# Spreading the reciprocal denominators by DMA in the linear-attention stage of a decoder layer

## The chip, the core and the metric

The kernel runs on one core of a Trainium2 chip. The metric is the device time of one launch in microseconds (us). Its engines are PE (matmuls, with the weight loads as PEld), DVE (vector), ACT (scalar), POOL (GpSimd) and SP, which here only issues DMAs. Each engine runs its own instructions in program order and waits on semaphores.

## The reference, cut to what matters

One decoder layer in fp32 on x of shape (2, 2048, 512): linear attention, cross attention over 154 context tokens, and a mixture of experts, each behind a layer norm and with a residual. The change touches the linear attention alone:

```python
qkv = x @ w_qkv                                   # 16 heads of 32
q_proj = _elu1(einsum('bhnd,hdf->bhnf', q, proj_matrix))     # 128 features
k_proj = _elu1(einsum('bhnd,hdf->bhnf', k, proj_matrix))
kv = einsum('bhnf,bhnd->bhfd', k_proj, v)
attn = einsum('bhnf,bhfd->bhnd', q_proj, kv)
z = 1.0 / (einsum('bhnf,bhf->bhn', q_proj, k_proj.sum(axis=2)) + 1e-08)
out = (attn * z[..., None]) @ w_out + b_out
x = x + out
```

The next stage's queries, `layernorm(x) @ Wq.T + bq`, are made in the same loop.

## The kernel before

Four stages follow each other: `project` (the projections and the sums over keys, up to about 424 us), `attend_linear` (424 to 742 us), `attend_cross` and `experts`. The tokens are cut into 8 blocks of 512 (`TB`); a block has 4 groups of 4 heads (`G`, `HG`). An fp32 product is made of three matmuls with parts called HI and LO (`PASSES`), so a tile of 128x512 over 512 inputs takes 12 matmuls.

`attend_linear` is a software pipeline written out by hand. `turns(slot)` calls every engine's `slot(i, s, ahead, now, behind)` for bodies i = -1 to 8 and slots s = 0 to 7. In body i three blocks are worked on: the features of block i+1 ("ahead"), the normalisation, output projection and layer norm of block i ("now"), and the cross-attention queries of block i-1 ("behind"). Each slot begins with two heads: PE makes a head's product in one of three banks (L1166), ACT makes relu and exp (L1003, L1006), DVE joins them (L1086). After its two heads PE runs the jobs that `PLAN[s]` lists:

- ND g (L1176, L1182): the denominators (`p_den`) and numerators (`p_num`) of a group of four heads. ND 3 of block i stands in slot 0 of body i; then all denominators of the block are there.
- R g (L1191, `spread_out`): the reciprocals, which lie in 16 of the 128 partitions, are spread over the 32 partitions of each head by a matmul with a matrix of ones and zeros, HI and LO.
- O t (L1204, `out_proj`): the output projection of 128 tokens, 12 matmuls; group g of its input needs `norm_lo` of that group.
- T t (L1213): four transposes of the layer-normed tokens.
- XQ g (L1226, `queries`): a 128-row part of the queries of block i-1, 12 matmuls.

R, O, T and XQ share three banks in the order in which they come; a job waits until the one three places before has been read. The denominators go: ACT copies them with 1e-8 added (`take_den`, L960), DVE takes the reciprocal in two halves (L1049), ACT and POOL split it into HI and LO (L965, L924), PE spreads it (R), DVE multiplies the numerators by it (`normalise`, L1054), ACT makes HI of the product (`normalised`, L971), POOL makes LO (L936, `norm_lo`), and O may begin.

A finished XQ g is read by ACT (`query`, L989) and DVE (L1091) into one of two buffers, `xq[:, g % 2]`, which SP writes to DRAM (`query_out`, L874). ACT's `query(m, g)` for g = 2 and 3 waits until the write of g - 2 of the same block has landed (`xq_out[g % 2]`). SP issues all DMAs of the loop, in its own program order: `query_out`, `load_q` (L186, the queries of the linear attention two blocks ahead), the store and the load of x.

## Time and profile before

| | us |
|---|---|
| median of 3 runs | 2382.08 |
| lowest, highest | 2378.66, 2383.08 |
| profiled execution | 2380.94 |
| its span | 2379.2 |
| PE busy in the span | 2278.0 |
| attend_linear in the span | about 424 to 742 |

The page gives each engine's busy time over the whole span; the views by stretch and the timeline give it for one body of the loop. A granted clock of 1.00 is TensorE's higher level (2.4 GHz), 0.50 its lower one (1.2 GHz). Times in a timeline are from the start of the span. A wait is put down to the event that came last.

### The profile page before, as it was taken

Reading aid. Unit: us, or ns where it says so; the run is one execution under the profiler, and the core shown is the slowest. Engines: PE = TensorE matmul, PEld = TensorE weight load, DVE = VectorE, ACT = ScalarE, POOL = GpSimd, SP = SyncE. Lnnn points to the kernel's source line nnn. Section 1 sums busy time; section 2 is a strip of 40 time slices with the busy share of each in tenths; the row PEclk is TensorE's granted clock in tenths of the full one; section 3 lists DMA queues with packets and bytes.
Section 4 is the critical chain, followed back from the end, with each engine's and each line's share of the span. In section 5 each row is a group of like instructions: output and inputs, shape, how many; then the busy total and the mean of one; then the engine's idle time right before and its main releaser. Section 6 shows DMA issues by size and latency. Waiting matters only on the chain.

```text
span 2379.2 us, 34267 instructions
## 1 busy us (share of the span) xinstructions
PE 2278.0 (96%) x12200; PEld 1775.7 (75%) x12200; DVE 1390.5 (58%) x2258; ACT 1158.5 (49%) x2745; POOL 838.9 (35%) x820
## 2 busy tenths in 40 slices
PE   7999999899998899998799999999999999999998
PEld 6888886566666566665588878888788887888887
DVE  5555456777774668777644466444664445644444
ACT  3555566767663767774544444333343333433332
POOL 1444345333341245545677762111111111111111
PEclk9999999999999899999899999999999999999999
DMA  7655546666646457784656546454345543464442
GB/s 209 161 146 128 134 107 157 210 187 195 177 142 181 102 145 188 185 225 138 217 174 212 177 141 214 171 177 142 129 153 201 177 142 125 136 215 139 140 139 77
DMA packets 140218, 387.46 MB, mean 163 GB/s; under 512 B 15920, under 2 KB 38064, under 8 KB 123440
## 3 DMA queue, kind: packets, MB, share of 16 engines
q1 hardware_dynamic: 139760, 384.77, 53.9%
q8 instruction: 98, 1.61, 0.3%
q10 hardware_dynamic: 288, 0.49, 0.1%
q14 instruction: 72, 0.59, 0.1%
HBM read 254.00 MB, written 104.07 MB: 151 GB/s over the span
## 4 chain that ended last, share of the span: by engine, by line
PE 51%; DVE 1%; issue 0%; ACT 0%; DVEq 0%
PE ex_pg L2593 32%; PE ex_pd L2609 18%; DVE ex_xb L2410 0%; PE ex_pd L2559 0%; PE ex_pd L2570 0%; DVE ex_up L2430 0%; DVE ex_acc L2447 0%; ACT ex_xb L2260 0%; DVE stage L2406 0%; DVE ex_ht L2439 0%; DVE ex_lg L2348 0%; DVE ex_rank L2382 0%; DVE ex_gt L2379 0%; DVE ex_rank L2380 0%; DVE ex_g L2423 0%
## 5 line engine op out<-in xcount | busy, mean ns | idle before, releaser
L2593 PE MATMUL ex_pg<-ex_xb,first_wg 128*128 128x512 f32 x3360 | 821.5, 391 | 12.0 <-DVE ex_up L2430 7.0
L2593 PEld LDWEIGHTS ex_pg<-ex_xb,first_wg 128*128 128x128 f32 x3360 | 632.0, 189 | 153.0 <-issue 15.7
L2609 PE MATMUL ex_pd<-ex_wd,ex_ht 128*128 128x512 f32 x1920 | 486.4, 389 | 2.9 <-issue 2.6
L2609 PEld LDWEIGHTS ex_pd<-ex_wd,ex_ht 128*128 128x128 f32 x1920 | 360.0, 188 | 79.1 <-issue 4.5
L2447 DVE SCALAR_TENSOR_TENSOR ex_acc<-ex_pd,ex_share,ex_acc 128x512 f32<-128x512 f32 x320 | 239.7, 749 | 302.4 <-PE ex_pd L2609 302.2
L2267 ACT COPY ex_m<-ex_pg 128x512 f32<-128x512 f32 x240 | 141.1, 588 | 383.5 <-PE ex_pg L2593 383.4
L2211 POOL TENSOR_TENSOR ex_h<-ex_g,ex_up 128x512 f32<-128x512 f32 x80 | 103.3, 1292 | 553.3 <-issue 458.2
L1590 ACT ACTIVATE cr_prob<-cr_s_bank,cr_top 128x154 f32<-128x154 f32 x512 | 194.7, 401 | 89.3 <-DVE cr_top L1700 86.6
L422 POOL TENSOR_TENSOR pr_ks_sum<-pr_ks_sum,pr_kp 128x512 f32<-128x512 f32 x128 | 165.2, 1291 | 161.6 <-DVE pr_kp L570 150.0
L2271 ACT ACTIVATE ex_g<-ex_g 128x512 f32<-128x512 f32 x160 | 101.3, 633 | 238.0 <-DVE ex_g L2423 165.5
L2203 POOL TENSOR_TENSOR ex_wd<-stage,ex_wd 128x512 fp32r<-128x512 f32 x80 | 105.8, 1343 | 260.1 <-ACT ex_wd L2248 260.1
L2278 ACT CAST ex_ht<-ex_h 128x512 fp32r<-128x512 f32 x160 | 99.4, 622 | 133.1 <-POOL ex_h L2211 133.0
L570 DVE SCALAR_TENSOR_TENSOR pr_kp<-pr_pk,pr_kp 128x512 f32<-128x512 f32 x128 | 88.5, 691 | 104.1 <-ACT pr_kp L475 103.4
L1700 DVE TENSOR_REDUCE cr_top<-cr_s_bank 128x3 f32<-128x462 f32 x192 | 110.4, 578 | 59.3 <-PE cr_s_bank L1865 59.2
L1865 PEld LDWEIGHTS cr_s_bank<-cr_k_w,cr_q 96*128 96x128 f32 x512 | 74.1, 199 | 77.1 <-issue 37.2
L2416 DVE TENSOR_TENSOR ex_g<-ex_pg,ex_m 128x512 f32<-128x512 f32 x80 | 55.3, 691 | 130.1 <-PE ex_pg L2593 124.9
L2439 DVE TENSOR_TENSOR ex_ht<-ex_h,ex_ht 128x512 fp32r<-128x512 f32 x160 | 122.2, 764 | 0.1
L1865 PE MATMUL cr_s_bank<-cr_k_w,cr_q 96*128 96x154 f32 x512 | 98.5, 302 | 20.1 <-DMA cr_q<-xq_scratch 11.9
L1590 ACT ACTIVATION_READ_ACCUMULATOR cr_prob<-cr_s_bank,cr_top 128x1 f32 x512 | 110.1, 215 | 0.0
L1927 PE MATMUL cr_bank<-cr_wo,cr_u 128*128 128x512 f32 x384 | 103.4, 407 | 4.0 <-DVE cr_x L1729 4.0
L1086 DVE SCALAR_TENSOR_TENSOR qp<-li_h_bank,qp 128x512 f32<-128x512 f32 x112 | 75.2, 681 | 46.7 <-ACT qp L1006 46.0
L473 ACT ACTIVATE pr_kp<-pr_pk 128x512 f32<-128x512 f32 x124 | 73.2, 590 | 52.8 <-PE pr_pk L702 52.8
(222 smaller groups left out, 3588.9 us busy)
## 6 DMA issues: line engine op xcount, KB each, us to landing
first_wg<-w_scratch SPq DMA_DIRECT2D x60, 1024.0 KB, 5.1
first_wg<-w_scratch SPq DMA_DIRECT2D x60, 768.0 KB, 4.3
w_scratch<-first_wg SPq DMA_DIRECT2D x20, 1792.0 KB, 6.8
stage<-in_units SPq DMA_DIRECT2D x60, 512.0 KB, 6.9
qk<-pr_kq SPq DMA_DIRECT2D x192, 128.0 KB, 2.4
qk<-q_scratch SPq DMA_DIRECT2D x96, 256.0 KB, 4.7
cr_q<-xq_scratch SPq DMA_DIRECT2D x96, 256.0 KB, 8.0
q_scratch<-pr_kq SPq DMA_DIRECT2D x128, 128.0 KB, 2.3
```

The costliest lines, as they stand in the source:

```text
L422: nc.gpsimd.tensor_tensor(part, part, slot(step), ALU.add).then_inc(ks_step, 1)
L1590: last = nc.scalar.activation(prob[:, n % 2, t, j, 0:KEYS], s_bank[(MU * n + v) % SBANKS][:, at * KEYS:(at + 1) * KEYS], ACT.Exp, bias=top ...
L1700: nc.vector.tensor_reduce(dst.rearrange("p t j -> p (t j)") if t == t_end else dst[:, :, 0], src, AX.X, ALU.max, negate=True).then_inc(top ...
L1865: mm = nc.tensor.matmul(s_bank[at % SBANKS][:, k * KEYS:(k + 1) * KEYS], q3[:, n % QRING, j, t * P:(t + 1) * P], k_w[:, n // G // BLK, j, ...
L1927: mm = nc.tensor.matmul(bank_of("O", m)[:], u[:, s, g, tile_cols(m)], wo[:, w, g], start=(n == 0), stop=(n == 3 * G - 1))
L2203: nc.gpsimd.tensor_tensor(wd[:, n % 2, LO, cols], d_raw[:, cols], wd[:, n % 2, HI, cols].bitcast(F32), ALU.subtract).then_inc(wd_lo, 1)
L2211: nc.gpsimd.tensor_tensor(h[:, f, 1], g[:, f, 1], up[:], ALU.mult).then_inc(h1_set, 1)
L2267: nc.scalar.copy(dst[:], pg[f][BANK[j]][:]).then_inc(m_set, 1)
L2439: nc.vector.tensor_tensor(ht[:, LO, f, k], h[:, f, k], ht[:, HI, f, k].bitcast(F32), ALU.subtract)\
L2447: nc.vector.scalar_tensor_tensor(acc[:, at], bank_of("D", n, i)[:], share[:, NT * half + at, e:e + 1], acc[:, at], ALU.mult, ALU.add).then ...
L2593: mm = nc.tensor.matmul(pg[f][BANK[j]][:], wg[:, f, j, s, c * P:(c + 1) * P], xb[:, j, m, c * TB:(c + 1) * TB], start=(k == 0 and j in FRESH),
L2609: mm = nc.tensor.matmul(bank_of("D", n, i)[:], ht[:, s, f, k, t * P:(t + 1) * P], wd[:, n % 2, m, f * D:(f + 1) * D], start=(at == 0), sto ...
```

## The change

The matmuls R and their HI and LO parts are gone. In their place SP writes the reciprocals of a block to a DRAM scratch, 4 rows of 512 for each of 4 partition groups, waits until they have landed, and reads them back with four DMAs that repeat a row for 32 partitions, into a new SBUF tile `rec` of 128x2048. DVE multiplies the numerators by `rec` in place of a bank. `spread_rec` stands in slot 1 of SP's program, ahead of `query_out` of the same slot. Further, XQ 3 moves from slot 6 to slot 3, O 0 from slot 3 to slot 4, and the rest of O follows it through slot 6; the divisions and their HI copies move from slot 2 to slot 3; layer-norm steps of DVE move with O. POOL waits at the start of the next stage until the last queries have landed.

```diff
     PLAN = {
         0: [("ND", 3), ("XQ", 0, 0, 12)],
         1: [("XQ", 1, 0, 12)],
-        2: [("R", 0), ("R", 1), ("R", 2), ("R", 3), ("XQ", 2, 0, 12)],
-        3: [("ND", 0), ("O", 0, 0, 12)],
-        4: [("O", 1, 0, 12), ("O", 2, 0, 6)],
-        5: [("ND", 1), ("O", 2, 6, 12), ("O", 3, 0, 12)],
-        6: [("XQ", 3, 0, 12), ("T", 0), ("T", 1)],
+        2: [("XQ", 2, 0, 12)],
+        3: [("ND", 0), ("XQ", 3, 0, 12)],
+        4: [("O", 0, 0, 12), ("O", 1, 0, 6)],
+        5: [("ND", 1), ("O", 1, 6, 12), ("O", 2, 0, 12)],
+        6: [("O", 3, 0, 12), ("T", 0), ("T", 1)],
         7: [("ND", 2), ("T", 2), ("T", 3)],
     }
...
+                def spread_rec(i):
+
+                    sp.wait_ge(recip_set, 2 * (i + 1))
+                    for j in range(HG):
+                        sp.dma_start(rec_dram[i, j * G:(j + 1) * G], den[j * HD:j * HD + G, 1]).then_inc(row_out, 16)
+                    sp.wait_ge(row_out, 16 * HG * (i + 1))
+                    if i:
+                        sp.wait_ge(divided, G * i)
+                    rows = rec_dram[i].rearrange("(j g) t -> j g t", j=HG)
+                    for j in range(HG):
+                        sp.dma_start(rec[j * HD:(j + 1) * HD], rows[j:j + 1].broadcast_to([HD, G, TB])).then_inc(rec_in, 16)
+
                 def slot(i, s, ahead, now, behind):
-                    if behind and s in (1, 2, 3, 7):
-                        query_out(i - 1, (1, 2, 3, 7).index(s))
+                    if now and s == 1:
+                        spread_rec(i)
+                    if behind and s in (1, 2, 3, 4):
+                        query_out(i - 1, s - 1)
...
-                    dve.wait_ge(r_full, G * i + g + 1)
-                    nc.vector.tensor_tensor(num[:, g], num[:, g], bank_of(i, "R", g)[:], ALU.mult).then_inc(r_taken, 1)
+                    dve.wait_ge(rec_in, 16 * HG * (i + 1))
+                    nc.vector.tensor_tensor(num[:, g], num[:, g], rec[:, g], ALU.mult).then_inc(divided, 1)
...
-                    if now and s == 2:
-                        for g in range(G):
-                            normalised(i, g)
-                    if behind and s == 2:
-                        query(i - 1, 2)
+                    if behind and s == 2:
+                        query(i - 1, 2)
+                    if behind and s == 3:
+                        query(i - 1, 3)
+                    if now and s == 3:
+                        for g in range(G):
+                            normalised(i, g)
...
             @block.gpsimd
             def _(pool):
+                for landed in xq_out:
+                    pool.wait_ge(landed, 16 * NB * BLK * G // 2)
```

On DVE, `reciprocal` of the next block waits also until the rows of this one have been written. In slot 3 DVE now runs the slot's first head, XQ 2's LO part, two divisions, the second head, and two divisions. In slot 6 it runs `add_out` 2, the first head, `norm` 1, the second head, `norm` 2, `add_out` 3, the LO parts of T 0 and T 1, and `norm` 3.

The order on PE, in a body with three blocks under work, from the slot that held R to the end of slot 4. Before:

```order
L1166 MATMUL li_h_bank<-qk,f_w 128x512 x2
L1191 MATMUL li_bank<-li_rec,li_spread 128x512 x8
L1226 MATMUL li_bank<-li_u_ln,wq 128x512 x12
L1166 MATMUL li_h_bank<-qk,f_w 128x512 x2
L1176 MATMUL li_p_den<-qp,ks_w 32x512 x4
L1182 MATMUL li_p_num<-qp,kv_w 32x512 x4
L1204 MATMUL li_bank<-li_wo,li_u_att 128x512 x12
L1166 MATMUL li_h_bank<-qk,f_w 128x512 x2
L1204 MATMUL li_bank<-li_wo,li_u_att 128x512 x18
```

And now, with `li_u_ln,wq` the queries XQ and `li_wo,li_u_att` the output projection O:

```order
L1160 MATMUL li_h_bank<-qk,f_w 128x512 x2
L1211 MATMUL li_bank<-li_u_ln,wq 128x512 x12
L1160 MATMUL li_h_bank<-qk,f_w 128x512 x2
L1170 MATMUL li_p_den<-qp,ks_w 32x512 x4
L1176 MATMUL li_p_num<-qp,kv_w 32x512 x4
L1211 MATMUL li_bank<-li_u_ln,wq 128x512 x12
L1160 MATMUL li_h_bank<-qk,f_w 128x512 x2
L1189 MATMUL li_bank<-li_wo,li_u_att 128x512 x18
```

The eight R matmuls are gone, XQ 3 stands where O 0 stood, and O 0 comes right behind the two heads of the next slot.

ACT in slots 2 and 3 of such a body, before (`li_u_att<-li_num` are the HI copies of the divided numerators, `li_xq` the query copies):

```order
L1003 ACTIVATE qp<-li_h_bank 128x512
L1006 ACTIVATE qp<-qp 128x512
L1003 ACTIVATE qp<-li_h_bank 128x512
L1006 ACTIVATE qp<-qp 128x512
L971 CAST li_u_att<-li_num 128x512 x4
L989 ACTIVATE li_xq<-li_bank,li_bq 128x512
L1003 ACTIVATE qp<-li_h_bank 128x512
L1006 ACTIVATE qp<-qp 128x512
L1003 ACTIVATE qp<-li_h_bank 128x512
L1006 ACTIVATE qp<-qp 128x512
L951 COPY li_num<-li_p_num 128x512
```

And now:

```order
L984 ACTIVATE li_xq<-li_bank,li_bq 128x512
L996 ACTIVATE qp<-li_h_bank 128x512
L999 ACTIVATE qp<-qp 128x512
L996 ACTIVATE qp<-li_h_bank 128x512
L999 ACTIVATE qp<-qp 128x512
L984 ACTIVATE li_xq<-li_bank,li_bq 128x512
L966 CAST li_u_att<-li_num 128x512 x4
L952 COPY li_num<-li_p_num 128x512
```

The four HI copies moved from ahead of the copy of XQ 2 to behind the copy of XQ 3.

SP in one body, now; before, the two rows with `rec_scratch` were not there and the fourth `xq_scratch` write stood behind the store of x:

```order
L904 DMA li_x<-in_x 128x4x512
L883 DMA rec_scratch<-li_den 4x512 x4
L889 DMA li_rec<-rec_scratch 32x2048 x4
L872 DMA xq_scratch<-li_xq 128x2x512 x2
L186 DMA qk<-q_scratch 32x2048 x3
L872 DMA xq_scratch<-li_xq 128x2x512 x2
L186 DMA qk<-q_scratch 32x2048 x6
L900 DMA x_scratch<-li_x 128x2048
```

All query writes of a body moved behind the eight DMAs of the reciprocals.

## Rows read from the trace of the kernel before

**Rows 1.** The page: its span.
```profile
span 2379.2 us, 34267 instructions
```

**Rows 2.** Busy time by stretch: bodies 0 to 3 of the linear stage.
```profile
core 0: us, PE busy (x) PEld busy (x) DVE busy (x) ACT busy (x) POOL busy (x), PEclk, DMA share, GB/s
424.28:459.23 34.95, 30.36 (x157) 18.14 (x153) 28.25 (x49) 26.75 (x46) 14.16 (x14) 0.90 0.45 124
...
537.85:577.40 39.55, 38.55 (x203) 25.42 (x202) 29.72 (x56) 28.39 (x52) 14.22 (x14) 1.00 0.65 186
```

**Rows 3.** Timeline of PE, body 3: start, length, line, idle before and releaser.
```profile
547.59 1.09 PE L1191 MATMUL li_bank<-li_rec,li_spread 128*128 128x512 f32 x4
...
550.70 3.04 PE L1226 MATMUL li_bank<-li_u_ln,wq 128*128 128x512 f32 x12 [0.46 <-DVE li_num L1054]
553.57 0.63 PE L1166 MATMUL li_h_bank<-qk,f_w 96*128 96x512 f32 x2
...
555.99 3.02 PE L1204 MATMUL li_bank<-li_wo,li_u_att 128*128 128x512 f32 x12
558.84 0.63 PE L1166 MATMUL li_h_bank<-qk,f_w 96*128 96x512 f32 x2
...
570.06 0.63 PE L1166 MATMUL li_h_bank<-qk,f_w 96*128 96x512 f32 x2
570.53 2.93 PE L1226 MATMUL li_bank<-li_u_ln,wq 128*128 128x512 f32 x12
```

**Rows 4.** Timeline of ACT and DVE, body 3.
```profile
550.27 1.65 ACT L971 CAST li_u_att<-li_num 128x512 fp32r<-128x512 f32 x3
553.83 0.69 ACT L989 ACTIVATE li_xq<-li_bank,li_bq 128x512 fp32r<-128x512 f32 x1 [0.74 <-PE li_bank L1226]
554.42 0.59 ACT L1003 ACTIVATE qp<-li_h_bank 128x512 f32<-128x512 f32 x1
556.73 0.57 ACT L951 COPY li_num<-li_p_num 128x512 f32<-128x512 f32 x1
...
543.58 1.74 DVE L1049 RECIPROCAL li_den<-li_den 128x256 f32<-128x256 f32 x1
561.24 0.68 DVE L1060 TENSOR_TENSOR li_x<-li_x,li_bank 128x512 f32<-128x512 f32 x1
563.02 0.68 DVE L1086 SCALAR_TENSOR_TENSOR qp<-li_h_bank,qp 128x512 f32<-128x512 f32 x1
```

**Rows 5.** Timeline of POOL, body 3.
```profile
550.95 5.03 POOL L936 TENSOR_TENSOR li_u_att<-li_num,li_u_att 128x512 fp32r<-128x512 f32 x4 [1.36 <-ACT li_u_att L971]
```

**Rows 6.** SP in the cross stage, where a like spreading runs.
```profile
796.91 0.31 SPq L1434 DMA_DIRECT2D rec_scratch<-cr_rec_row  x1
798.49 1.73 SPq L1440 DMA_DIRECT2D cr_rec<-rec_scratch  x4
```

**Rows 7.** DMA issues of 745 to 1160 us: size, median us from issue to landing.
```profile
cr_rec<-rec_scratch SPq DMA_DIRECT2D x32, 256.0 KB, 5.0
rec_scratch<-cr_rec_row SPq DMA_DIRECT2D x8, 32.0 KB, 1.6
```

**Rows 8.** The query writes, L874: landing, and who waited for them.
```profile
  ACT li_xq L989: 2.1, 1
DMA to landing us min/median/max: 2.7/3.4/7.8
```

**Rows 9.** The timelines of bodies 0 and 7: DVE's second reciprocal or both, PE's O.
```profile
429.09 1.74 DVE L1049 RECIPROCAL li_den<-li_den 128x256 f32<-128x256 f32 x1
439.12 3.01 PE L1204 MATMUL li_bank<-li_wo,li_u_att 128*128 128x512 f32 x12
...
699.15 3.37 DVE L1049 RECIPROCAL li_den<-li_den 128x256 f32<-128x256 f32 x2 [0.71 <-ACT li_den L960]
710.60 11.48 PE L1204 MATMUL li_bank<-li_wo,li_u_att 128*128 128x512 f32 x48
```

**Rows 10.** Busy time by stretch in body 0, columns as in rows 2.
```profile
430.00:432.00 2.00, 0.57 (x1) 0.29 (x1) 1.38 (x2) 1.33 (x4) 0.66 (x1) 0.77 0.89 193
432.00:434.00 2.00, 2.00 (x6) 1.49 (x5) 1.24 (x2) 1.97 (x4) 2.00 (x3) 0.50 0.01 0
```

More of the change, by code:

```diff
@@ L810, in attend_linear @@
         u_ln = sb("u_ln", [P, 2, C, TB], F32R)
-        spread = sb("spread", [P, G, P], F32R)
-        rec = sb("rec", [P, 2, TB], F32R)
+        rec = sb("rec", [P, G, TB])
         bias = sb("bias", [P, D])
@@ L969, in normalised @@
                         act.wait_ge(o_full, TT * i) if i else None
[L970 removed]
+                    act.wait_ge(divided, G * i + g + 1)
                     nc.scalar.copy(u_att[:, HI, g], num[:, g]).then_inc(norm_hi, 1)
@@ L998, in slot @@
                             take_den(i)
-                        if now and s == 1 and h == PER + 1:
-                            reciprocal_high(i, 1)
                         slot_free(act, n)
@@ L1015, in slot @@
                         take_num(i, G - 1)
-                    if now and s == 0:
-                        reciprocal_high(i, 0)
                     if behind and s == 0:
                         query(i - 1, 0)
-                    if now and s == 1 and not ahead:
-                        reciprocal_high(i, 1)
                     if behind and s == 1:
                         query(i - 1, 1)
-                    if now and s == 2:
+                    if behind and s == 2:
[3 more added lines that the diff above has]
+                    if now and s == 3:
                         for g in range(G):
                             normalised(i, g)
-                    if behind and s == 2:
-                        query(i - 1, 2)
                     if (ahead or i == -1) and s in (3, 5):
                         take_num(i + 1, (s - 3) // 2)
-                    if behind and s == 6:
-                        query(i - 1, 3)
                     if now and s == 6:
@@ L1103, in slot @@
                     if s == 6 and now:
-                        add_out(i, 3)
+                        add_out(i, 2)
                     if s == 2 and behind:
                         query(i - 1, 1)
-                    if s == 2 and now:
-                        normalise(i, 0)
                     first()
@@ L1115, in slot @@
                         reciprocal(i, 0)
-                    if s == 2 and now:
+                    if s == 3 and now:
+                        normalise(i, 0)
                         normalise(i, 1)
+                    if s == 4 and behind:
+                        query(i - 1, 3)
+                    if s == 6 and now:
+                        norm(i, 1)
+                    second()
+                    if s == 3 and now:
                         normalise(i, 2)
+                        normalise(i, 3)
                     if s == 4 and now:
                         add_out(i, 0)
+                    if s == 5 and now:
+                        add_out(i, 1)
+                        norm(i, 0)
                     if s == 6 and now:
                         norm(i, 2)
-                    if s == 6 and behind:
-                        query(i - 1, 3)
-                    second()
-                    if s == 2 and now:
-                        normalise(i, 3)
-                    if s == 6 and now:
-                        norm(i, 3)
                     if i == -1 and s == 0:
@@ L1142, in slot @@
                             .then_inc(wq_lo, 1)
-                    if s in (4, 5) and now:
-                        add_out(i, s - 3)
-                        norm(i, s - 4)
-                    if s in (6, 7) and now:
-                        turned(i, 2 * s - 12)
-                        turned(i, 2 * s - 11)
+                    if s == 6 and now:
+                        add_out(i, 3)
+                        turned(i, 0)
+                        turned(i, 1)
+                        norm(i, 3)
+                    if s == 7 and now:
+                        turned(i, 2)
+                        turned(i, 3)
                 turns(slot)
@@ L1184, in attend_group @@
                     mm.then_inc(num_full, 1)
-                def spread_out(i, g):
-                    bank_free((i, "R", g))
-                    if g == 0:
-                        pe.wait_ge(rec_set, 2 * (i + 1))
-                    for s in (HI, LO):
-                        mm = nc.tensor.matmul(bank_of(i, "R", g)[:], spread[:, g], rec[:, s], start=(s == HI),
-                                              stop=(s == LO))
-                    mm.then_inc(r_full, 1)
                 def out_proj(i, t, lo, hi):
@@ L1237, in slot @@
                             continue
-                        {"XQ": queries, "ND": attend_group, "R": spread_out, "O": out_proj, "T": transposes}[job[0]](
+                        {"XQ": queries, "ND": attend_group, "O": out_proj, "T": transposes}[job[0]](
                             m, *job[1:])
```

44 lines of the change are left out of this document (14 added, 30 removed).

## The prediction

> **What bounds the kernel now.** Look first at the span [rows 1], then at the busy time by body of the linear stage [rows 2]. A steady body takes 39.55 us, and PE is busy for 38.55 of them at a granted clock of 1.00; DVE has 29.72, ACT 28.39, POOL 14.22. So PE sets the pace here, and a matmul taken from it counts, provided that what comes next is ready. The timeline of PE in body 3 [rows 3] shows what the change touches: R stands from 547.59 to 550.70, the start of XQ 2, so 3.11 us with its small waits. The other engines have room in their sums, but each runs in order, so the question is which chain reaches O 0.
>
> **What it removes.** R goes in 8 bodies: 8 x 3.11 = 24.9 us at most. ACT's and POOL's splitting of the reciprocals goes too; neither is a bound, and I count it as nothing, since neither ran late for O before.
>
> **What the new order costs at O 0, even with a DMA that takes no time.** Slots 2 and 3 together hold the same work as before but for R, because XQ 3 is as long as O 0 (12 matmuls, 555.99 to 558.84 is 2.85). In body 3's clock slot 4 therefore would start at 558.84 - 3.11 = 555.73. Two heads alone take 0.47 (570.06 to 570.53), so without a wait O 0 would end at 555.73 + 0.47 + 2.85 = 559.05. But ACT now copies XQ 3 before it makes the HI copies of the divided numerators, and POOL's LO copies come after those. ACT begins a query copy 0.26 behind the start of the next slot (553.83 against 553.57), spends 0.59 on it [rows 4], and POOL starts 0.68 after ACT's first HI copy (550.95 against 550.27) and needs 5.03 for four [rows 5]. PE's last three matmuls of O 0 take 0.72 (3 of 12 in 2.85). That is 555.73 + 0.26 + 0.59 + 0.68 + 5.03 + 0.72 = 563.0, a wait of 3.95 us where 3.11 were won. Before, POOL's four ran from 550.95 to 555.98, beside XQ 2 and ND 0, and O 0 began at 555.99: they were just hidden. Now that cover is gone. This part of the wait is certain from the order of ACT alone.
>
> **What the DMAs add.** DVE ends the second reciprocal at 543.58 + 1.74 = 545.32. SP then issues four row writes. Four issues took 1.73 us in the like spreading of the cross stage [rows 6], so the last one starts 1.3 later, at 546.6. Such a write landed in 1.6 us [rows 7], at 548.2. Until then SP stands, and behind it in its queue stand `query_out` 0 and 1 and `load_q`. The four reads occupy SP to 550.0, and a like read landed in 5.0 us [rows 7], the last at about 553.5. That alone would be early enough for the divisions. `query_out` 0, for which XQ 0 is ready in slot 1, now goes out only at 550.0. Its landing took 2.7 to 7.8 us, 3.4 in the middle [rows 8]. I take 5.0, the figure of the reads, as it now has 1 MB ahead of it: 555.0. The bounds are 552.7 and 557.8.
>
> On that landing hangs more than it seems. ACT's copy of XQ 2 must wait for it, as the buffer is the same; XQ 2 itself is complete by 553.57 - 3.11 = 550.5 now, against 553.6 before, when this wait cost 2.1 us once in the whole stage [rows 8]. And behind ACT's waiting instruction stand both heads of slot 3, the copy of XQ 3 and all four HI copies. From 555.0: the copy 0.59, two heads 2.31 (554.42 to 556.73), the second copy 0.59 [rows 4], then 0.68, 5.03 and 0.72 as above: 564.9; DVE's own order (head, XQ 2's LO part, first division) adds about 0.1. O 0 ends at 565.05 and not 559.05: a wait of **6.0 us**. PE's heads of slot 4 need a bank that ACT and DVE free late, which lies inside the same wait. With the landing at 552.7 the wait falls to the 3.95 of the order; at 557.8 it is 8.8.
>
> Two smaller terms. In slot 6, O 3 now ends right ahead of the transposes, and DVE has between T 0 and `norm` 3 one `norm` (0.55 taken, a 128x512 pass as short as ACT's), one `add_out` (561.24 to 563.02, 1.78) and two LO parts of T (0.6 each from start to start; L1060's pass lasts 0.68). Slot 6 starts at 570.06 and body 4 at 577.4, 7.36 later; by DVE's list T 3 would end 8.5 after the slot's start, of which some 0.4 was lost before anyway at the first heads: 0.7 us, between 0 and 1.2. And a PE that waits can lose its clock: in body 0 it was nearly idle from 430 to 432 (0.57 busy), and the next 2 us were granted 0.50, the lower level [rows 10]. A new idle of some 5 us per body is as long, but the low stretch falls mostly on matmuls that wait for POOL anyway; 0.5 us, between 0 and 2.
>
> Per body with three blocks (bodies 1 to 6): -3.11 + 6.0 + 0.7 + 0.5 = **+4.1**, six times 24.6.
>
> **Body 0** has no queries, so the landing of `rec` itself decides. The second reciprocal ends at 429.09 + 1.74 = 430.83 [rows 9]; rows landed 2.9 later, 433.7; last read issued at 435.1, landed at 440.1; division 0.6, 0.68 to POOL, 5.03, 0.72: O 0 ends at 447.1. It ended at 439.12 + 2.85 = 441.97; the heads that followed it now lie ahead (0.47), and the clock, low after a wait this long, adds some 0.8: **+5.5**.
>
> **Body 7** has no heads. Reciprocals end at 699.15 + 3.37 = 702.52 [rows 9]; by the same steps `query_out` 0 goes out at 707.2 and lands at 712.2. Copy 0.59, DVE's LO part and division 1.3, 0.68, 5.03, 0.72: 720.5. O 0 could have ended at 710.60 - 3.0 + 2.75 + 2.85 = 713.2. So 7.3 of waiting, less 3.0 for R, and 0.6 at the transposes: **+5**.
>
> **The sum.** 24.6 + 5.5 + 5 = 35 us on the profiled execution's 2380.94, whose span is 2379.2; the median lies 1.1 above that execution. 2382.08 + 35 = 2417.
>
> **Where the Trainium skill speaks.** Of two transfers from one queue, the rows show only landings: 3.4 us for a query write alone, 5.0 for the reads [rows 7, 8]. "DMA: Bandwidth & Descriptors", section "Queues, rings and completion order", says that each DMA engine takes up descriptors in the order of its ring, so a write issued behind 1 MB of reads waits for them. By that the landing is nearer to 557.8 than to 553.4, and the sum nearer to +50 than to +23; no row of before has this pair. On the clock, the low stretch after body 0's idle is measured [rows 10]; "TensorE: Matmul & The Clock Gate", section "HAM oscillation — how this bites in real kernels", describes an engine that waits for a DMA at every tile and starts each one at the lower clock. By that rule the low clock would come back in every body, the last rival below.
>
> **The rivals.**
> 1. The query write lands by 552.7 and the reads faster than 5 us. Then only ACT's order and POOL's pace are left: -3.11 + 3.95 + 0.4 is +1.2 in six bodies, +4 in body 0, +2.5 in body 7, together +14: 2396. For it: 2.7 us has been seen. Against: 1 MB stands ahead. Chance 0.17.
> 2. The other side, faster: POOL's pass is cheaper than 5.03 for four shows, POOL's times being rough on the page. It stands at O 0, ahead of the first matmuls. If a pass took 0.6 us, like ACT's copies (1.65 for three), and the query write landed by 552.7, O 0 would end at 555.73 + 0.26 + 0.59 + 4 x 0.55 + 0.7 + 0.72 = 560.2, a wait of 1.15; per body -2, six times -12, with +4 in body 0 and -1 in body 7: -9, 2373. It decides from a pass of about 1.0 us down. Against it: O 0 before began within 0.01 of POOL's end and the passes lie back to back. Chance 0.07. Near it, a sum within the measurement: 0.05.
> 3. The low clock comes back in every body and lies on O 1 rather than under the wait: up to 2 us more per body, 35 + 13 = 48, 2430; with a landing at 557.8 as well, 2445. Chance 0.10.
> The forecast itself, the landing between 553.5 and 557 and the chain through ACT: chance 0.61.
>
> **How the numbers follow.** The predicted time is that of the likeliest case, 2417. The range goes down to 2392, into rival 1 whose time is 2396, and up to 2440, most of rival 3. About 0.2% (4.8 us) is what a measurement of this kernel can tell from no change. Faster 0.07, within it 0.05, slower 0.88.
>
> **What would show it.** In the timeline of after: R's matmuls gone; PE idle ahead of O (`li_bank<-li_wo,li_u_att`), 5 to 7 us per body, ended by POOL's `li_u_att`; ACT idle about 4 us ahead of the copy of XQ 2, ended by the DMA `xq_scratch<-li_xq`; POOL's four LO copies still 5.0 us; a steady body of 43.6 us against 39.55; body 0 of some 40 against 34.95 [rows 2]; O 0's wait there ended by `rec`. It is wrong if ACT waits for PE's XQ 3 instead (rival 1), if POOL's passes shrink (rival 2), or if DVE's waits for `rec` are the long ones in bodies 1 to 6, which would mean that the reads land later than I took.

## The result, and the profile after

The changed kernel takes 2445.4 us (median of 4, 2445.37 to 2445.98) against 2380.85 for the kernel before beside it (2378.66 to 2383.08): a ratio of 1.0272, interval 1.0254 to 1.0289. That is slower, as forecast, but by 64.5 us and not 35: outside the range.

The page's span, which answers to [rows 1]:

```profile
span 2443.6 us, 34184 instructions
```

Of the profiled executions' difference, 64.4 us, all and a little more lies in `attend_linear`. The table holds body lengths, worked out from the timeline of ACT as the distance from one `take_den` to the next; the column "end" runs from the `take_den` of body 7 to the start of the last XQ matmul, the column "rest" from there to the end of the span.

```
body        0      1      2      3      4      5      6    end    sum     rest
before  35.73  39.09  39.66  39.41  39.53  39.53  39.32  42.16  314.4  1638.6
after   44.50  54.38  48.84  46.35  45.61  46.38  45.19  53.34  384.6  1633.2
change   +8.8  +15.3   +9.2   +6.9   +6.1   +6.8   +5.9  +11.2  +70.2   -5.4
```

In all kernels of this study the rest lies between 1632.2 and 1638.6 us, with no order that follows their edits, and the stage begins between 425.7 and 427.9. I take both as scatter; what causes it was not looked into.

Busy time by stretch after (columns as in [rows 2]): body 0, body 1, body 3, and the 2 us behind PE's long wait in body 3.

```profile
424.00:468.40 44.40, 32.90 (x148) 17.19 (x145) 30.39 (x49) 27.32 (x46) 15.36 (x12) 0.81 0.45 108
468.40:522.80 54.40, 39.24 (x196) 24.94 (x194) 31.86 (x56) 27.81 (x49) 13.40 (x12) 0.84 0.73 213
571.60:618.00 46.40, 39.34 (x196) 25.16 (x194) 31.89 (x56) 27.82 (x49) 13.39 (x12) 0.93 0.68 182
...
596.00:598.00 2.00, 2.00 (x5) 1.11 (x6) 1.87 (x2) 0.72 (x2) 2.00 (x2) 0.50 0.00 0
```

R's matmuls are gone, but PE is no less busy in body 3 (39.34 against 38.55 us): what is left of its work runs partly at the lower clock. And it is idle for 7 us of 46.4, where it was idle for 1.

The timeline of PE in body 3 shows where, as [rows 3] does for before:

```profile
588.79 0.39 PE L1160 MATMUL li_h_bank<-qk,f_w 96*128 96x512 f32 x1
592.38 0.49 PE L1160 MATMUL li_h_bank<-qk,f_w 96*128 96x512 f32 x1 [3.19 <-DVE qp L1077]
595.77 7.25 PE L1189 MATMUL li_bank<-li_wo,li_u_att 128*128 128x512 f32 x18 [2.90 <-POOL li_u_att L937]
...
617.60 0.63 PE L1198 MATMUL li_bank<-ident,li_xn 128*128 128x128 f32 x4 [0.91 <-DVE li_xn L1065]
```

A wait of 3.19 us at a head, one of 2.90 at O 0, and then O 0 and half of O 1 in 7.25 us; the next head starts at 602.86. ACT over the same time:

```profile
589.76 0.69 ACT L984 ACTIVATE li_xq<-li_bank,li_bq 128x512 fp32r<-128x512 f32 x1 [6.22 <-DMA xq_scratch<-li_xq]
...
593.67 1.16 ACT L966 CAST li_u_att<-li_num 128x512 fp32r<-128x512 f32 x2 [0.35 <-DVE li_num L1045]
596.21 0.62 ACT L966 CAST li_u_att<-li_num 128x512 fp32r<-128x512 f32 x1 [1.38 <-DVE li_num L1045]
597.90 0.62 ACT L966 CAST li_u_att<-li_num 128x512 fp32r<-128x512 f32 x1 [1.06 <-DVE li_num L1045]
```

This is the chain that was forecast: the copy of XQ 2 waits for the write of XQ 0, and all behind it waits along. What was not forecast are the waits of 1.38 and 1.06 for DVE's divisions of groups 2 and 3. DVE and POOL:

```profile
592.90 1.28 DVE L1045 TENSOR_TENSOR li_num<-li_num,li_rec 128x512 f32<-128x512 f32 x2
594.10 0.68 DVE L1077 SCALAR_TENSOR_TENSOR qp<-li_h_bank,qp 128x512 f32<-128x512 f32 x1
594.70 3.17 DVE L1045 TENSOR_TENSOR li_num<-li_num,li_rec 128x512 f32<-128x512 f32 x2
...
594.36 5.88 POOL L937 TENSOR_TENSOR li_u_att<-li_num,li_u_att 128x512 fp32r<-128x512 f32 x4 [10.82 <-ACT li_u_att L966]
```

Two divisions take 1.28 us before POOL has begun, and the next two, of the same form, 3.17 while POOL works. POOL's four take 5.88 instead of the 5.03 of [rows 5]. Before, DVE's fourth division of body 3, which read a bank, also ran beside POOL's copies, and neither was longer for it:

```profile
551.76 0.68 DVE L1054 TENSOR_TENSOR li_num<-li_num,li_bank 128x512 f32<-128x512 f32 x1
```

SP's queue in bodies 3 and 1:

```profile
578.27 1.25 SPq L883 DMA_DIRECT2D rec_scratch<-li_den  x4
580.67 1.70 SPq L889 DMA_DIRECT2D li_rec<-rec_scratch  x4
582.41 0.94 SPq L872 DMA_DIRECT2D xq_scratch<-li_xq  x2
...
471.65 1.16 SPq L915 DMA_DIRECT2D stage<-in_WoT  x1
475.05 1.28 SPq L883 DMA_DIRECT2D rec_scratch<-li_den  x4
485.46 1.70 SPq L889 DMA_DIRECT2D li_rec<-rec_scratch  x4
487.20 0.94 SPq L872 DMA_DIRECT2D xq_scratch<-li_xq  x2
```

In body 3 SP can go on 1.15 us after the last row write is issued (579.52 to 580.67). The write of XQ 0 goes out at 582.41 and ACT is released at about 589.7, 7.3 us later. In body 1 the same rows take 9.1 us (476.33 to 485.46), since three loads of 1 MB (`WkT`, `WvT`, `WoT`, issued from 470.59 on for the next stage) are still under way. Over the whole stage, the waits with their sums, times and longest:

```profile
ACT li_xq L984 <- DMA xq_scratch<-li_xq: 52.9, 8, 14.7
...
PE li_bank L1189 <- POOL li_u_att L937: 31.9, 10, 7.5
...
PE li_h_bank L1160 <- DVE qp L1077: 29.9, 8, 11.6
...
DVE li_num L1045 <- DMA li_rec<-rec_scratch: 5.0, 1, 5.0
```

The first of these was 2.1 us, once, before [rows 8]. The reciprocals themselves are late only once, in body 0; elsewhere they lie ready while everybody waits for a query write behind them.

### The profile page after: what moved, and what is told of

The parts are those of the page before. It is cut to its first block, busy times and chain, and to the rows that moved or that the text cites. A ratio compares the mean times of both kernels' runs of the same rounds, so it can differ in the third digit from the quotient of the medians.

```text
span 2443.6 us, 34184 instructions
## 1 busy us (share of the span) xinstructions
PE 2284.4 (93%) x12136; PEld 1772.7 (73%) x12136; DVE 1406.6 (58%) x2257; ACT 1153.4 (47%) x2729; POOL 834.7 (34%) x804
## 4 chain that ended last, share of the span: by engine, by line
PE 49%; DVE 1%; issue 0%; ACT 0%; DVEq 0%
PE ex_pg L2580 31%; PE ex_pd L2596 18%; DVE ex_xb L2397 0%; PE ex_pd L2546 0%; PE ex_pd L2557 0%; DVE ex_up L2417 0%; DVE ex_acc L2434 0%; ACT ex_xb L2247 0%; DVE stage L2393 0%; DVE ex_ht L2426 0%; DVE ex_lg L2335 0%; DVE ex_rank L2369 0%; DVE ex_rank L2368 0%; DVE ex_rank L2367 0%; DVE ex_g L2410 0%
## 5 line engine op out<-in xcount | busy, mean ns | idle before, releaser
L1189 PE MATMUL li_bank<-li_wo,li_u_att 128*128 128x512 f32 x384 | 116.9, 457 | 32.3 <-POOL li_u_att L937 31.9
L1189 PEld LDWEIGHTS li_bank<-li_wo,li_u_att 128*128 128x128 f32 x384 | 80.1, 219 | 70.3 <-issue 38.5
```

The costliest lines, as they stand in the source:

```text
L1189: mm = nc.tensor.matmul(bank_of(i, "O", t)[:], u_att[:, s, g, t * P:(t + 1) * P], wo[:, m, g], start=(n == 0), stop=(n == MM - 1))
```

## The experiments

All ratios are to the kernel before on the same chip. The changed kernel did not run beside the experiments, so a difference to its 2445.4 compares two chips; the kernel before had medians of 2378.7 to 2380.9 on all of them. "Steady" is the length of bodies 3 to 6, from the table's measure: 39.4 before, 45.9 after.

### One part of the change at a time

**e4_order_alone** is the kernel before, R and all, with only the new order of XQ and O on PE and of the work that follows it; the HI copies of the numerators stay in slot 2.

```diff
-        3: [("ND", 0), ("O", 0, 0, 12)],
-        4: [("O", 1, 0, 12), ("O", 2, 0, 6)],
+        3: [("ND", 0), ("XQ", 3, 0, 12)],
+        4: [("O", 0, 0, 12), ("O", 1, 0, 6)],
...
```

> The kernel before with R and its matmuls kept, but XQ 3 in slot 3, O from slot 4 on, and DVE's layer-norm steps as in the changed kernel; ACT's HI copies stay in slot 2. Theory (the move of PE's jobs by itself costs only the later transposes): per body 0.7 to 1.1 us at T 3, nothing at O 0, together 5 to 9 us over before, about 2386 to 2390. Rival (the move itself costs much, since XQ 3 no longer covers DVE's sums): over 2 us per body, 2397 or more.

It took 2386.05 us, 1.0031 (1.0020 to 1.0042); steady 40.0. The new order by itself costs 0.6 us per body, near the 0.7 that I took for the transposes.

**e5_order_and_copies** adds the one other thing that the new order brings: the HI copies behind ACT's copy of XQ 3. Still with R, still no DMA.

```diff
-                    if now and s == 2:
-                        for g in range(G):
-                            normalised(i, g)
...
                     if behind and s == 3:
                         query(i - 1, 3)
+                    if now and s == 3:
+                        for g in range(G):
+                            normalised(i, g)
```

> The previous experiment (R kept, no spreading by DMA, the jobs of PE in the new order), and in addition ACT's HI copies in slot 3 behind the copy of XQ 3, as in the changed kernel; DVE's divisions stay in slot 2. Theory (ACT's order takes away the cover of POOL's four LO copies): 3.5 to 4 us more per body at O 0 than with the early copies, where 39.5 us bodies had become 40.1: 43.5 to 44, and in all some 28 to 34 us over the previous one, 2414 to 2420. Rival (POOL's copies start early enough, so the order of ACT costs little): bodies under 42 and a time below 2400.

It took 2422.5 us, 1.0184 (1.0169 to 1.0200), 36.5 above e4: a little over what was expected. Bodies 1 to 6 grew by 4.1 to 4.2 us each; the prediction had worked out 3.95. The timeline of PE and POOL, body 3:

```profile
578.66 5.97 PE L1209 MATMUL li_bank<-li_wo,li_u_att 128*128 128x512 f32 x18 [2.31 <-POOL li_u_att L936]
...
577.25 4.99 POOL L936 TENSOR_TENSOR li_u_att<-li_num,li_u_att 128x512 fp32r<-128x512 f32 x4 [10.77 <-ACT li_u_att L971]
```

POOL's four copies are as long as before (but for one of 2.85 us in body 0, taken up below), and PE runs after them: 2.31 us of open wait, and 18 matmuls in 5.97 us that take 4.36 when all is ready (e7 below). **Moving four short copies on ACT by one slot, behind the two query copies and the two heads between, costs more than half of the whole loss, with no DMA in it.**

**e12_no_spreading** asks what R was worth. It is the kernel before without R; the numerators are multiplied by a constant instead of the reciprocals.

```diff
-        2: [("R", 0), ("R", 1), ("R", 2), ("R", 3), ("XQ", 2, 0, 12)],
+        2: [("XQ", 2, 0, 12)],
...
-                    dve.wait_ge(r_full, G * i + g + 1)
-                    nc.vector.tensor_tensor(num[:, g], num[:, g], bank_of(i, "R", g)[:], ALU.mult).then_inc(r_taken, 1)
+                    dve.wait_ge(rec_set, 2 * (i + 1))
+                    nc.vector.tensor_scalar(num[:, g], num[:, g], half[:, 0:1], None, ALU.mult).then_inc(r_taken, 1)
```

> The kernel before without R and with nothing in its place: the reciprocals are made but not spread, and DVE multiplies the numerators by a constant, so the outputs are not the reference's. It prices what the removal of R could give at most. Theory (R is worth its 3.11 us per body on PE, since PE is the bound): steady bodies 36.4 to 36.7, in all about 25 us under the kernel before, 2352 to 2357. Rival (without R the DVE, ACT and POOL chain to O 0 or to the transposes decides, and POOL's LO copies come too late): steady bodies 38 or more, 2365 or above.

It took 2369.81 us, 0.9956 (0.9939 to 0.9972): 9.4 us less, and a steady body of 37.8, 1.7 less. I had expected 25 from a spreading that costs nothing. PE and POOL, body 3:

```profile
551.16 0.96 PE L1204 MATMUL li_bank<-li_wo,li_u_att 128*128 128x512 f32 x3 [0.28 <-POOL li_u_att L936]
552.41 0.96 PE L1204 MATMUL li_bank<-li_wo,li_u_att 128*128 128x512 f32 x3 [0.29 <-POOL li_u_att L936]
...
546.98 5.38 POOL L936 TENSOR_TENSOR li_u_att<-li_num,li_u_att 128x512 fp32r<-128x512 f32 x4 [1.36 <-ACT li_u_att L971]
```

With R gone, O meets POOL's LO copies group by group, POOL being the next limit right behind PE; the end also grew from 42.2 to 44.2. The stand-in is not neutral: DVE's products by a constant take 0.47 to 1.11 us each in this body, and POOL's four beside them 5.38 instead of 5.03. Without these 0.35 us a steady body would win some 2.0, an estimate. So in this kernel's order a spreading that took no time of PE's at all could win about 10 us (0.4%), or about 12 by that estimate.

### The write of XQ 0

**e1_four_buffers** is the changed kernel with four query buffers, so that no copy waits for a write of its own block.

```diff
-        xq = sb("xq", [P, 2, 2, TB], F32R)
+        xq = sb("xq", [P, G, 2, TB], F32R)
...
-                    if m or g >= 2:
-                        act.wait_ge(xq_out[g % 2], 16 * (2 * m + g // 2))
+                    if m:
+                        act.wait_ge(xq_out[g % 2], 16 * 2 * m)
```

> The changed kernel with four query buffers in place of two, so that ACT's copies of XQ 2 and XQ 3 no longer wait for a query write of the same block. Theory (the landing of the query write holds ACT, and behind it the heads and the HI copies): the ACT wait on xq_scratch, 52.9 us in 8, goes; then ACT's HI copies start behind XQ 3 or behind the landing of the spread reciprocals, some 3.3 us earlier in a steady body and more in body 1; 2445 falls to about 2415 to 2422. Rival (the reads of the reciprocals land as late as the write did, so DVE's division waits in ACT's place): DVE waits for rec by some 3 us or more per body and the time stays above 2435.

It took 2414.96 us, 1.0150 (1.0135 to 1.0165), 30 us less than the changed kernel; steady 41.4. The wait for the write and what hung on it is 4.5 us in a steady body, and more in bodies 1 and 2 (49.3 and 43.5 for 54.4 and 48.8).

**e9_write_before_reads** keeps two buffers and moves only the issue of the write of XQ 0: behind the row writes, ahead of the wait for them and of the four reads.

```diff
                         sp.dma_start(rec_dram[i, j * G:(j + 1) * G], den[j * HD:j * HD + G, 1]).then_inc(row_out, 16)
+                    if i:
+                        query_out(i - 1, 0)
                     sp.wait_ge(row_out, 16 * HG * (i + 1))
```

> The changed kernel with one move in SP's queue: the write of XQ 0 of the block stands between the four row writes and the wait for them, ahead of the four reads. Theory (ACT's copy of XQ 2 waits because that write is queued behind 1 MB of reads): the write lands some 4 us earlier and ACT's copy of XQ 2 no longer waits 6.2 us; but the write of XQ 1 still goes out behind the reads, and ACT's copy of XQ 3 waits for it. The heads of slot 3 come free; steady bodies 43 to 45 in place of 46, 2425 to 2437. Rival (the write is slow in itself, 7 us wherever it stands): ACT's copy of XQ 2 starts as late as before, time within 3 us of 2445.

It took 2423.95 us, 1.0185 (1.0171 to 1.0199), 21.5 less than the changed kernel. SP and ACT, body 3:

```profile
571.58 0.38 SPq L872 DMA_DIRECT2D xq_scratch<-li_xq  x1
572.06 2.18 SPq L891 DMA_DIRECT2D li_rec<-rec_scratch  x4
...
575.17 0.69 ACT L986 ACTIVATE li_xq<-li_bank,li_bq 128x512 fp32r<-128x512 f32 x1 [0.61 <-DMA xq_scratch<-li_xq]
580.86 0.69 ACT L986 ACTIVATE li_xq<-li_bank,li_bq 128x512 fp32r<-128x512 f32 x1 [2.69 <-DMA xq_scratch<-li_xq]
```

Issued ahead of the reads, the write is down 3.6 us after its issue, not 7.3. The price moves to the next write, XQ 1, which now stands behind the reads and holds up the copy of XQ 3 by 2.69 us. This pair shows what no row of before had: a write lands 3.7 us later when 1 MB of reads stands ahead of it in the same queue. The reads follow it by 0.5 us in e9, so the traffic is the same and only the order differs. "DMA: Bandwidth & Descriptors" of the Trainium skill, section "Queues, rings and completion order", has the rule, that an engine takes up descriptors in the order of its ring; the trace agrees.

### DVE and POOL

**e3_low_on_vector** takes POOL's LO copies away and gives them to DVE, behind the four divisions.

```diff
-                        nc.gpsimd.tensor_tensor(u_att[:, LO, g], num[:, g], u_att[:, HI, g].bitcast(F32), ALU.subtract)\
-                            .then_inc(norm_lo, 1)
...
+                        nc.vector.tensor_tensor(u_att[:, LO, g], num[:, g], u_att[:, HI, g].bitcast(F32), ALU.subtract)\
+                            .then_inc(norm_lo, 1)
```

> The changed kernel with the LO copies of the divided numerators made by DVE and not by POOL. Theory (DVE's division, both operands in SBUF now, slows to some 1.6 us a pass while POOL works, and POOL's pass is slow itself): all 32 divisions take 0.68 us, none 1.6; the four LO copies take 2.4 us and not 5.0 to 7.9; O 0 ends 2 to 3 us earlier per body; 2425 to 2432. Rival (the long divisions come from DMA traffic into rec or out of num): they stay long with POOL idle, and the time gains under 1 us per body, 2438 or more.

It took 2442.02 us, 1.0265 (1.0248 to 1.0282): 3.4 less, where more was expected. But the durations did what the theory said. The divisions by tile, count, and ns lowest/middle/highest, first in the changed kernel:

```profile
L1045 DVE TENSOR_TENSOR li_num<-li_num,li_rec x32: 681/689/1768, 440.2 to 775.2; 128x512 f32<-128x512 f32 x32
```

and in e3:

```profile
L1041 DVE TENSOR_TENSOR li_num<-li_num,li_rec x32: 680/683/692, 441.9 to 773.4; 128x512 f32<-128x512 f32 x32
```

Without POOL beside it no division lasts over 692 ns; with it they go up to 1768, and all 32 keep DVE busy for 34.7 us instead of 20.5. So DMA traffic into `rec`, the rival, is not the cause. Why the time hardly fell, the timeline of e3 shows, DVE and PE in body 3:

```profile
591.61 1.28 DVE L1041 TENSOR_TENSOR li_num<-li_num,li_rec 128x512 f32<-128x512 f32 x2
592.81 2.49 DVE L1045 TENSOR_TENSOR li_u_att<-li_num,li_u_att 128x512 fp32r<-128x512 f32 x4
...
593.64 5.84 PE L1192 MATMUL li_bank<-li_wo,li_u_att 128*128 128x512 f32 x18 [3.86 <-DVE li_u_att L1045]
```

All LO copies are done 2.5 us after the divisions, yet the 18 matmuls take 5.84 us instead of 4.36. They run after a long idle of PE, and the stage's granted clock is as low as in the changed kernel, 0.88.

**e2_filler** tests the clock alone: PE does 25 matmuls on tiles at hand where it would wait (13 behind XQ 3, 12 ahead of O 0), into the bank that O 0 then starts afresh.

```diff
+                    for _ in range(12 if t == 0 and lo == 0 else 0):
+                        nc.tensor.matmul(bank_of(i, "O", t)[:], wo[:, HI, 0, 0:P], wo[:, HI, 1], start=True, stop=True)
...
+                        for _ in range(13):
+                            nc.tensor.matmul(bank_of(i + 1, "O", 0)[:], wo[:, HI, 0, 0:P], wo[:, HI, 1], start=True,
+                                             stop=True)
```

> The changed kernel with 25 filler matmuls per body whose result is overwritten: 13 behind XQ 3 and 12 behind the heads of slot 4, all ahead of O 0. Theory (a good part of the loss is the lower clock on O 0 and O 1 after the idle time): although PE has more to do, the granted clock stays at 1.00 in the steady bodies, the 18 matmuls from O 0 on take 4.3 to 5.5 us and not 6.9 to 7.3, and the time falls by 10 to 20 us, to 2425 to 2435. Rival (the 18 matmuls are slow since they follow POOL's four passes): clock at 1.00 but the same end of O, time within 3 us of 2445 or above it.

It took 2446.19 us, 1.0280 (1.0265 to 1.0295). The clock came back, 0.96 over 424 to 800 us where the changed kernel has 0.88, and the time stayed. PE and POOL, body 3:

```profile
597.55 0.97 PE L1191 MATMUL li_bank<-li_wo,li_u_att 128*128 128x512 f32 x3
599.24 0.96 PE L1191 MATMUL li_bank<-li_wo,li_u_att 128*128 128x512 f32 x3 [0.72 <-POOL li_u_att L937]
...
596.20 5.91 POOL L937 TENSOR_TENSOR li_u_att<-li_num,li_u_att 128x512 fp32r<-128x512 f32 x4 [12.17 <-ACT li_u_att L966]
```

At the full clock each group of three matmuls waits for the next LO copy. The first three groups start 1.69 us apart, the pace of POOL's two middle copies (1.73 and 1.72 us).

**e7_low_on_vector_filler** does both: e3's edit and e2's.

> Both earlier edits together: LO copies by DVE, and the 25 filler matmuls ahead of O 0. Alone the filler gave nothing, and the LO copies by DVE 3.4 us. Theory (two limits lie on each other: POOL's slow passes and the low clock, either alone hides the other): together they give more than the sum, the 18 matmuls from O 0 on take 4.3 us, steady bodies fall to 43 to 44, the time to 2425 to 2432. Rival (the clock costs nothing here): within 3 us of 2442.

It took 2429.93 us, 1.0215 (1.0197 to 1.0233). The filler alone changed the time by +0.8, the LO copies on DVE by -3.4, the two together by -15.5. (Its four executions lie between 2426.6 and 2435.4, and the profiled one is the longest; the interaction is clear of that.) PE, body 3:

```profile
589.73 4.36 PE L1194 MATMUL li_bank<-li_wo,li_u_att 128*128 128x512 f32 x18 [1.02 <-DVE li_u_att L1045]
```

So the slow passes of POOL and DVE and the low clock lie over each other. To the start of the next head, the 18 matmuls and their waits take 7.1 us with both, 6.8 with the passes left (e2), 5.7 with the clock left (e3), and 4.2 with neither (e7).

**e10_four_buffers_vector** is e1 with the LO copies on DVE.

> The changed kernel with four query buffers and with the LO copies on DVE, ACT's order left as it is. Against four buffers alone (2415, steady bodies 41.6) it prices POOL's four passes where nothing else waits. Theory: O 0 ends some 4 x (1.26 - 0.6) = 2.6 us earlier per body; steady bodies 39 to 39.5, 2395 to 2400. Rival (the landing of the reciprocals is the limit there, and POOL only follows it): steady bodies above 41, 2410 or more.

It took 2406.35 us, 1.0117 (1.0103 to 1.0131), 9 less than e1: between what the theory and the rival said. Steady is 40.9. With the query write out of the way, DVE waits for the reciprocals in all 8 bodies, 20.3 us in sum, where the changed kernel had 5.0 in one. But 16.8 of these lie in bodies 0, 1 and 7; in bodies 2 to 6 it is 0.5 to 0.9, and there PE still waits some 2 us for the LO copies, behind ACT's order.

### The weight loads, and a mended kernel

**e6_loads_after** moves the three 1 MB loads of body 0's last slot behind body 1's spreading.

```diff
-                    if i == 0 and s == 7:
+                    if i == 1 and s == 5:
```

> The changed kernel with the three weight loads of 1 MB each (WkT, WvT, WoT) issued in body 1, slot 5, and not in body 0, slot 7, ahead of the first row writes of body 1. Theory (body 1 is 6 to 8 us longer than the steady ones because its four row writes land behind 3 MB of loads): the row writes of body 1 land in 2 us in place of some 9, body 1 falls from 54.4 to about 47, the rest stays: 2437 to 2439. Rival (the excess of body 1 is the clock or the first use of the queries): body 1 stays above 52 and the time within 2 us of 2445.

It took 2444.26 us, 1.0276: no gain. Body 1 fell from 54.4 to 46.5 us, as it should if the loads delayed the rows; body 2 rose from 48.8 to 51.0. By the profiled execution the bodies sum to 6.2 us less, but the stage began 1.9 later and the rest took 3.5 more, both inside the scatter named above, and the medians differ by 1.1. So the loads are shown to be what makes body 1 long, but not that the time can be had back by moving them. Body 2 shows where it went: the store of x, now behind the loads, was issued at 512.32 and landed 10.2 us later, the rows behind it went out at 523.01 and took 4.0 us from the last issue instead of 1.15, and ACT waited 10.3 us for the write of XQ 0, where the changed kernel's body 2 had 6.2.

**e8_all_mended** puts together four buffers, the LO copies on DVE right behind each division, the HI copies ahead of the copy of XQ 3 again, the loads of e6, and `norm` 3 ahead of a LO part of the transposes.

> The changed kernel with every wait found so far taken out: four query buffers, ACT's HI copies ahead of the copy of XQ 3, LO copies by DVE between the divisions, the weight loads later, and norm 3 ahead of the LO part of T 1. Theory (R is worth 3.1 us per body once nothing waits for what replaced it): steady bodies of 37.5 to 39, body 0 still some 5 us longer as nothing covers the landing of the reciprocals there; 2372 to 2384, near or a little below the kernel before. Rival (the round trip through DRAM is too long for O in slot 4 whatever is mended): DVE waits for rec in every body, steady bodies above 39.5, 2386 to 2395.

It took 2396.62 us, 1.0073 (1.0059 to 1.0086): still slower than before, against the expectation. Bodies 3 to 5 are 39.0 to 39.7 long, no better than before with R; body 6 takes 41.2, and body 2 45.5. SP's queue there:

```profile
504.51 0.34 SPq L900 DMA_DIRECT2D x_scratch<-li_x  x1
...
515.11 0.39 SPq L904 DMA_DIRECT2D li_x<-in_x  x1
515.54 1.42 SPq L883 DMA_DIRECT2D rec_scratch<-li_den  x4
521.13 2.27 SPq L889 DMA_DIRECT2D li_rec<-rec_scratch  x4
```

The store of x, now behind the loads, lands 10 us after its issue; SP waits for it before it loads the next x, and the rows stand behind that.

**e11_mended_loads** issues the loads earlier, at `i == 1 and s == 2`.

> The kernel of e8 with the three weight loads in body 1, slot 2, right behind the reads of the reciprocals, so that neither the store of x nor the row writes of the next body stand behind them. Theory (body 2 was 45.5 us there since the store of x took 10 us to land behind the loads and SP waited): body 2 falls to 39 to 41; 2390 to 2393, still above the kernel before by body 0 and the last bodies. Rival: body 2 stays above 44 and the time at 2396.

It took 2396.69 us, 1.0076 (1.0062 to 1.0089): the same median. In the profiled executions the bodies sum to 4.6 us less (body 2 fell to 42.2, the end grew from 47.8 to 49.0), which single executions, 2395.6 to 2400.7 here and 2394.2 to 2400.6 in e8, don't confirm. Against before it is mostly the ends that lose: body 0 takes 5.0 us more and the last part 6.9, bodies 1 and 2 take 1.8 and 2.5 more, and bodies 3 to 6 are level (39.3 against 39.4). So with the waits mended that had been found, the DMA's way costs the ends and wins nothing in between. Waits are left: DVE waits for the reciprocals in all 8 bodies, 13.7 us in sum (19.0 in e8, as its rival had said), though under 1.0 us in bodies 3 to 6, and in body 3 PE waits 1.0 us for the LO copies and 0.45 at the transposes. No version with the DMA beat the kernel before.

## Why the prediction was wrong in size

The direction, the place and the chain held: O 0 waits for POOL, POOL for ACT's HI copies, ACT for its copy of XQ 2, and that for the write of XQ 0. Each step by its number:

- **R's worth**, 8 x 3.11 us. In the new order no run shows it alone: e5, with R, is 44.2 long, and e1, without R or the write's wait but with POOL's slower copies, 41.4, so 2.8 went in net, which does not speak against it. But as the size of what there was to win it was wrong: e12 gave 1.7 per body and 9.4 in all. I had read in [rows 3, 5] that O 0 began within 0.01 us of POOL's end, and did not use it to say that PE's saving ends there.
- **The order on ACT**, 3.95 us per body: measured 4.2 (e5 less e4). Right.
- **The transposes**, 0.7: measured 0.6 (e4), and a wait of 0.91 at T 3. Right.
- **The landing of the write of XQ 0.** Forecast: issue 12.1 us into the body, landing 5.0 later, at 17.1. Measured: issue 10.8, landing 7.3 later, at 18.1. I took the reads' 5.0 us [rows 7], and had the upper bound of 7.8 from [rows 8] and the Trainium skill's rule for it; the rule was right, and e9 shows it. The landing alone was 2.3 us too short; that only 1.0 us per body came of it is luck, as the issue was put 1.3 too late. Within this step the last read should also have landed at 554.5 by its own terms (548.2, 1.3 to the last issue, 5.0), and not at 553.5; the sum does not use it.
- **What the change does to DVE and POOL: left out.** The division now reads both operands from SBUF, where it read one from a bank. Against 0.6 us for a division and 5.03 for POOL's four, they took up to 1.77 and, in body 3, 5.88. "SBUF — State Buffer" of the Trainium skill, section "Who interferes with whom", says just this: a DVE instruction with two SBUF inputs contends with a GpSimd instruction that reads SBUF. I had not weighed it. The trace agrees, with 1.28 us for two divisions ahead of POOL's work and 3.17 for two beside it, and e3 with none over 692 ns. The times fit that each waits until the other's pass has ended: in body 3 DVE's third and fourth division end 0.56 and 0.54 us after POOL's first and second copy, and POOL's second and third copy 1.14 and 1.15 us after those divisions. No run tests it further.
- **The clock**, 0.5 per body: the low clock is there, 0.50 in the stretch 596 to 598, under the 18 matmuls that take 7.25 us. But it can't be given a number of its own: e2 brought it back and won nothing, since POOL's pace was then the limit. The last rival, the low clock in every body, is there in the trace, and its upper time, 2445, is even the measured one; but that is a coincidence of sums, as the excess lies in body 1 and in the terms above.

In body 3 the two heads behind O 1's first half start 31.2 us into the body; by the prediction's steps they would at 28.6. Of the 2.6 us, 1.0 is the landing, 0.4 the HI copies that wait on DVE, 0.85 POOL's slower passes, and about 0.4 what the matmuls behind them lose at the low clock. So bodies 3 to 6 lost 6.4 on average and not 4.1, and together they account for 9.3 us of the miss.

**Body 1 was the largest single miss**, 15.3 instead of 4.1. The three 1 MB loads stand in the same queue ahead of the rows, in before's program too, and I gave one price to six bodies without looking at what SP issues in each. With the rows 9.1 us on their way instead of 1.2, ACT's wait was 14.7 us. Body 2 lost 9.2 instead of 4.1. PE's waits there are those of body 3 within 0.3 us, but the 18 matmuls behind them take 9.5 us to the start of the next head, where body 3 has 7.1, with a further wait of 0.57 for POOL in their middle:

```profile
546.89 4.93 PE L1189 MATMUL li_bank<-li_wo,li_u_att 128*128 128x512 f32 x9 [2.60 <-POOL li_u_att L937]
552.40 4.21 PE L1189 MATMUL li_bank<-li_wo,li_u_att 128*128 128x512 f32 x9 [0.57 <-POOL li_u_att L937]
...
545.48 6.86 POOL L937 TENSOR_TENSOR li_u_att<-li_num,li_u_att 128x512 fp32r<-128x512 f32 x4 [12.20 <-ACT li_u_att L966]
...
548.91 2.30 DVE L1129 TENSOR_SCALAR stage<-stage 128x2048 f32<-128x2048 f32 x1
```

That is 2.4 of the 2.5 us by which body 2 is longer than body 3. In this body alone DVE scales a weight tile for the next stage (`stage`, L1129), and POOL's fourth LO copy, beside it, takes 2.26 us instead of 1.28; the first nine matmuls take 0.8 more for it. The last nine take 1.6 more: the granted clock is 0.50 under all of them, where in body 3 it was back at 1.00 for the last seven. Why the low clock lasts longer in body 2 stays open. **Body 0** lost 8.8 instead of 5.5, with `rec` late as forecast (DVE waits 5.0 us), and POOL's four took 7.92 us instead of 5.03. Of these the fourth alone took 3.32, beside a long pass of DVE's that makes the LO part of `wq`:

```profile
445.03 3.37 DVE L1133 TENSOR_TENSOR wq<-stage,wq 128x2048 fp32r<-128x2048 f32 x1
```

Before, this pass ran at 441.93, when O 0 had already begun; the change moved the LO copies onto it. In e5, whose divisions read a bank, POOL's first copy met the same pass and took 2.85. **The end** lost 11.2 instead of 5:

```profile
776.50 13.94 PE L1189 MATMUL li_bank<-li_wo,li_u_att 128*128 128x512 f32 x48 [7.51 <-POOL li_u_att L937]
...
792.19 0.66 PE L1198 MATMUL li_bank<-ident,li_xn 128*128 128x128 f32 x4 [0.87 <-DVE li_x L1051]
795.12 0.63 PE L1198 MATMUL li_bank<-ident,li_xn 128*128 128x128 f32 x4 [2.28 <-DVE li_xn L1065]
```

The wait of 7.51 is the forecast's 7.3. But the 48 matmuls behind it take 13.94 us instead of the 11.48 of [rows 9], at a granted clock of 0.50 up to about 782, and the transposes wait 3.15. The misses of the bodies, 3.3 + 11.2 + 5.1 + 9.3 + 6.2, are the 35 us between the 35 forecast and the 70.2 measured in the stage; the rest of the program took 5.4 us off again.

Which leaves the step that failed: "What the DMAs add", and the one price of +4.1 per body that it led to, "six times 24.6". It took 1.6 us for the landing of the rows in every body; in body 1, behind the loads, they took 9.1, and that body makes 11.2 us of the miss. It took 5.0 for the landing of the query write, measured 7.3, and 5.03 for POOL's four copies, measured 5.88 and more, since what the new operands do to DVE and POOL had no term. The low clock had one, of 0.5, and the matmuls under it lost 1.6 us more in body 2 than in body 3, and took 13.94 us instead of 11.48 at the end. Still open is why the low clock lasts longest in body 2.

## What to carry to other kernels

Before a stage of the bounding engine is taken away, look for the engine that ends just with it: here POOL's four copies ended 0.01 us before PE's next work, so 3.1 us of matmuls were worth 1.7. Where an in-order engine or queue gets a new wait, price all that stands behind it and all that stands ahead of it in each iteration, including those in which something rare (weight loads) goes out. And where an operand moves from a bank to SBUF, look who else reads SBUF at that time.

## What the runs showed of the hardware

- A 128x512 fp32 product of two SBUF tiles takes DVE 0.68 us alone and up to 1.77 beside POOL's subtractions of SBUF tiles, and POOL's passes go from 1.26 us to 1.72 beside it. With one operand in a bank, in the kernel before, the two ran beside each other at 0.68 and 1.30. POOL's longest passes stood beside longer ones of DVE's: 2.26 beside a scaling of 128x2048 (2.30), 3.32 beside a subtraction of 128x2048 (3.37).
- A 512 KB write in the queue behind four reads of 256 KB lands 7.3 us after its issue, ahead of them 3.6 (e9, also body 3). Behind three loads of 1 MB, four writes of rows of 8 KB each need 9.1 us from the last issue instead of 1.2.
- Behind two waits of 3.19 and 2.90 us, with 0.5 us of work between them, matmuls ran at a granted clock of 0.50, in a stretch in which PE was busy throughout (2.00 of 2.00 us). Filling the waits with other matmuls gave 0.96 over the stage and no time, as long as the operands came at POOL's pace.
